# Storing the context's two half-precision parts in the first attention and loading them in the last stage

## What is computed

```python
x = x + jnp.tanh(g_xattn[0]) * _L0_xattn_ref(_layernorm(x, axis=-1), ctx_4096, L0_xattn_Wq, L0_xattn_Wk, L0_xattn_Wv, L0_xattn_Wo)
x = x + jnp.tanh(g_ffn[0]) * _L0_ffn_ref(_layernorm(x, axis=-1), L0_ffn_weight_scales, L0_ffn_weight_q)
x = x + jnp.tanh(g_xattn[1]) * _L1_xattn_ref(_layernorm(x, axis=-1), ctx_4096, L1_xattn_Wq, L1_xattn_bq, L1_xattn_Wk, L1_xattn_bk)
x = x + jnp.tanh(g_ffn[1]) * _L1_ffn_ref(_layernorm(x, axis=-1), L1_ffn_W, L1_ffn_b, L1_ffn_A, L1_ffn_B, L1_ffn_gate_w, L1_ffn_gate_b)
```

## Time and profile before

| | us |
|---|---|
| median of 3 runs (lowest, highest) | 2219.08 (2218.75, 2219.87) |
| the profiled execution | 2214.46 |
| its span, first to last instruction | 2212.6 |
| TensorE busy in the span | 2039.8 (92%) |
| VectorE, ScalarE, GpSimd busy | 1093.4, 774.5, 705.7 |
| `ctx_raw` loads | 32 of 1500.0 KB |
| HBM read, written | 170.49 MB, 51.65 MB |

### The profile page before, as it was taken

The page is one execution under the profiler, slowest core; times in us unless marked ns, Lnnn a source line. Parts: engine busy times, 40 slices in busy tenths (PEclk is TensorE's granted clock), DMA queues, the critical chain, the costliest instruction groups (busy, mean ns, idle before and its releaser), DMA issues. The chain is left out here.

```text
span 2212.6 us, 33544 instructions
## 1 busy us (share of the span) xinstructions
PE 2039.8 (92%) x11792; PEld 1189.2 (54%) x11792; DVE 1093.4 (49%) x2004; ACT 774.5 (35%) x1552; POOL 705.7 (32%) x708
## 2 busy tenths in 40 slices
PE   7989999997999999999999959999999847999998
PEld 3456666654555556555555524444444425665665
DVE  4544444454455555545555633344344427566554
ACT  3422222221455555555555621111111124334431
POOL 0000000011455556555556520000000035665752
PEclk9999999999999999999999979999999969999999
DMA  5423333334124222242222352232232165565561
GB/s 170 143 85 92 88 88 90 87 96 103 35 71 102 63 59 62 62 103 65 62 62 67 97 157 62 61 86 71 57 85 72 64 180 175 184 205 187 172 215 52
DMA packets 331369, 223.21 MB, mean 101 GB/s; under 512 B 295152, under 2 KB 301040, under 8 KB 327072
## 3 DMA queue, kind: packets, MB, share of 16 engines
q1 hardware_dynamic: 244224, 195.36, 31.0%
q10 hardware_dynamic: 87072, 26.89, 5.1%
HBM read 170.49 MB, written 51.65 MB: 100 GB/s over the span
## 5 line engine op out<-in xcount | busy, mean ns | idle before, releaser
L816 POOL TENSOR_TENSOR b_probT<-b_exp,b_probT 128x448 f16<-128x448 f32 (+2 forms) x256 | 265.4, 1040 | 308.8 <-ACT b_probT L879 308.8
L404 POOL TENSOR_TENSOR cT<-ctx_raw,cT 128x375 f16<-128x375 f32 x256 | 220.2, 881 | 135.4 <-ACT cT L399 135.4
L634 PE MATMUL a_pr<-proj_q_p,a_yT 128*128 128x384 f16 x1344 | 228.5, 329 | 2.5 <-DVE a_yT L554 2.5
L946 DVE TENSOR_REDUCE b_nmax<-b_mx_ps 112x2 f16<-112x974 f32 x128 | 149.6, 1168 | 123.9 <-PE b_mx_ps L1027 123.9
L1015 PE MATMUL b_kv_ps<-wkv_p,cT 128*128 128x384 f16 (+1 forms) x1152 | 210.8, 325 | 0.0
L1011 PE MATMUL b_kv_ps<-cT,wkv_p 128*128 128x375 f16 x1152 | 199.6, 324 | 9.0 <-PEq L412 9.0
L1052 PE MATMUL b_s_ps<-b_qT,b_kT 96*128 96x448 f16 (+5 forms) x768 | 188.9, 353 | 2.2 <-DMA b_qT<-b_nrow 2.2
L1067 PE MATMUL b_o_ps<-b_probT,b_v 128*128 128x448 f16 (+5 forms) x768 | 187.3, 351 | 3.1 <-POOL b_probT L816 3.1
L877 ACT ACTIVATE b_exp<-b_s_ps 128x448 f32<-128x448 f32 (+2 forms) x256 | 138.1, 540 | 143.6 <-PE b_s_ps L1052 137.5
L634 PEld LDWEIGHTS a_pr<-proj_q_p,a_yT 128*128 128x128 f16 x1344 | 130.3, 99 | 87.1 <-issue 5.9
L1702 PE MATMUL d_f_ps<-d_w_p,d_y3T 128*112 128x512 f16 x768 | 175.8, 383 | 0.0
(11 more groups left out here) (191 smaller groups left out, 2977.6 us busy)
## 6 DMA issues: line engine op xcount, KB each, us to landing
ctx_raw<-in_ctx_t SPq DMA_DIRECT2D x32, 1500.0 KB, 7.8
d_cn_raw<-in_ctx_nat SPq DMA_DIRECT2D x32, 512.0 KB
qk_scratch<-a_heads ACTq DMA_DIRECT2D x28, 480.0 KB, 6.5
b_qT<-qk_scratch SPq DMA_DIRECT2D x32, 336.0 KB, 4.1
o_scratch<-b_o SPq DMA_DIRECT2D x128, 84.0 KB, 1.9
c_oT<-o_scratch SPq DMA_DIRECT2D x28, 384.0 KB, 5.0
d_cn_raw<-in_ctx_nat SPq DMA_DIRECT2D x16, 476.0 KB
x_scratch<-c_x SPq DMA_DIRECT2D x14, 512.5 KB, 4.6
```

The costliest lines, as they stand in the source:

```text
L404: pool.tensor_tensor(cT[:, p, 1, k, 0:S], ctx_raw[:, k, :], cT[:, p, 0, k, 0:S], ALU.subtract).then_inc(split_lo, 1)
L634: last = mm(pr[:, c % 3, 0:KW], yT[:, p, a, k, :], weight(b, k, c), start=(n == 0 and k == 0), stop=(n == 2 and k == KD - 1))
L816: pool.tensor_tensor(pT[0:m, c, 1, :], ex[0:m, i % 2, :], pT[0:m, c, 0, :], ALU.subtract).then_inc(p_lo, 1)
L946: dve.tensor_reduce(nmax[:, 2 * t:2 * t + 2], mx_ps[0:Q, :, 0:SA], AX.X, ALU.max, negate=True).then_inc(topped, 1)
```

## The change

A scratch array `ct_s` of the shape (batch, partition, part, chunk, 375) in fp16 is added. In stage b, SyncE begins each slot with `store_parts`: once batch b is split it writes both parts of its `cT` buffer to `ct_s` (1.5 MB). ScalarE and GpSimd wait for that store before they write the split of batch b+2 into the same buffer. In stages c and d nothing of the context is split for `cT`: `load_parts` reads the two fp16 parts of a batch from `ct_s` straight into `cT`, for batches 0 and 1 at the head of stage c, and for batch s+1 in slot s of stage d, behind a wait for the scores of batch s-1, which read that buffer last. TensorE waits for that load (`ct_loaded`) where it waited for `split_lo`.

```diff
@@ stage b @@
+                    def load_parts(sp, p, b):
+                        sp.dma_start(cT[:, p, :, :, 0:S].rearrange("p l k s -> p (l k) s"),
+                                     ct_s[bass.ds(b, 1), :, :, :, :].rearrange("b p l k s -> p (b l k) s")).then_inc(ct_loaded[p], 16)
...
+                        def store_parts(j, p, b):
+                            sp.wait_ge(split_lo, KD * (b + 1))
+                            sp.dma_start(ct_s[bass.ds(b, 1), :, :, :, :].rearrange("b p l k s -> p (b l k) s"),
+                                         cT[:, p, :, :, 0:S].rearrange("p l k s -> p (l k) s")).then_inc(ct_stored[p], 16)
                         def slot(j, p, b):
+                            store_parts(j, p, b)
                             load_row(p, b, 1)
...
                             if k == 0:
                                 wait(pool, kv_done, 6 * (b - 1))
+                                pool.wait_ge(ct_stored[p], 16 * (j + 1))
...
@@ stage c @@
                     load(0, 1, 1)
+                    for b in range(2):
+                        load_parts(sp, b, b)
...
-                        if isinstance(s, int) and s == SLOTS - 2:
-                            load_raw(sp, B, 0)
...
-                        if isinstance(s, int) and s == SLOTS - 2:
-                            for k in range(KD):
-                                split_low(pool, 0, B, k)
...
@@ stage d @@
-                load_raw(sp, B + 1, 1)
...
-                            load_raw(sp, s + 1 + B, s + 1)
+                            sp.wait_ge(scored, s)
+                            load_parts(sp, 1 - p, s + 1)
                             load_rows(1 - p, s + 1)
...
-                    if inside(s + 1, B):
-                        for k in range(KD):
-                            split_low(pool, 1 - p, s + 1 + B, k)
...
-                    if inside(s + 1, B):
-                        wait(act, scored, s)
-                        for k in range(KD):
-                            split_high(act, 1 - p, s + 1 + B, k)
...
-                        pe.wait_ge(split_lo, KD * (s + 1 + B))
+                        pe.wait_ge(ct_loaded[p], 16 * (j + 1))
```

More of the change, by code:

```diff
@@ L114, in build @@
     x2_s = nc.dram_tensor("x2_scratch", [R, D + 4], F32).ap()
+    ct_s = nc.dram_tensor("ct_scratch", [B, P, 2, KD, S], F16).ap()
     w4_s = nc.dram_tensor("w4_scratch", [P, KD * D], BF16).ap()
@@ L384, in build @@
                     raw_loaded = nc.alloc_semaphore(name="b_raw_loaded")
+                    ct_stored = [nc.alloc_semaphore(name=f"b_ct_stored{i}") for i in range(2)]
+                    ct_loaded = [nc.alloc_semaphore(name=f"d_ct_loaded{i}") for i in range(2)]
                     split_hi, split_lo = nc.alloc_semaphore(name="b_split_hi"), nc.alloc_semaphore(name="b_split_lo")
@@ L802, in _, with split_piece @@
                             sp.wait_ge(o_stored[i], 32 * B * KV // 2)
+                            sp.wait_ge(ct_stored[i], 16 * B // 2)
                     @block.gpsimd
                     def _(pool):
-                        def split_piece(p, b, k):
+                        def split_piece(j, p, b, k):
                             if k == 0:
                                 wait(pool, kv_done, 6 * (b - 1))
+                                pool.wait_ge(ct_stored[p], 16 * (j + 1))
                             split_low(pool, p, b, k)
@@ L837, in slot @@
                                 if SPLIT_AT <= i < SPLIT_AT + KD and inside(b + 2, B):
-                                    split_piece(p, b + 2, i - SPLIT_AT)
+                                    split_piece(j, p, b + 2, i - SPLIT_AT)
                         run_slots(pool, slot, B)
@@ L844, in _, with split_piece @@
                     def _(act):
-                        def split_piece(p, b, k):
+                        def split_piece(j, p, b, k):
                             if k == 0:
                                 wait(act, kv_done, 6 * (b - 1))
+                                act.wait_ge(ct_stored[p], 16 * (j + 1))
                             split_high(act, p, b, k)
@@ L1227, in slot @@
                             act.activation(y2T[:, 0, :], tr32, ACT.Copy).then_inc(y2T_hi, 1)
-                        if isinstance(s, int) and s == SLOTS - 2:
-                            for k in range(KD):
-                                split_high(act, 0, B, k)
                     run_slots(act, slot, SLOTS, 4)
```

## The result

The changed kernel takes 2229.52 us (median of 5 runs, 2227.41 to 2232.87) against 2219.08 us (5 runs, 2217.76 to 2223.2): ratio 1.0045, 95% interval 1.003 to 1.006. Timed again beside 27 runs of the kernel before it gave 1.0033, 1.0019 to 1.0046. So it is slower by 7 to 10 us, above the range of the prediction (2211.5 to 2225.0), and its sign is wrong. The profiled execution shown here is 15.5 us longer than the one of before (2229.97 to 2214.46); its span is 2228.2.

A forecast was written before the change was run, and what follows sets the result against it. TensorE was taken to bound the kernel: busy through stage b, held by its own gaps in d. Terms -1.7 - 1.0 + 0.1 = -2.6 us took the median 2219.08 to 2216.5 us, with a range of 2211.5 to 2225.

The forecast's parts named there:

- (1): Stages c and d: removing sixteen second splits, beside TensorE's work, is worth 0 in c and in steady slots of d.
- (2): Stage d, slot 9: TensorE's wait for `d_y` goes, as the root is done earlier; worth 1.7 us.
- (3): Stage d, slot 2: the collision stays, but root, subtractions and `d_y` come sooner; worth 1.0 us.
- (5): Stage d: loading `cT` in 750-byte runs takes 4.4 us, 0.8 more (ends 0 and 2.7); costs 0.1 us in slot 3.
- (6): Stage b: each slot's store takes 4.4 to 6.2 us, within 7.1 us of cover before ScalarE reads `ctx_raw`; worth 0.
- slow-store rival: Stage b: a store over 7.1 us loses the excess in each of 14 slots, up to 2259 us; chance 0.05.
- (4): Start of stage d: 1.5 MB less to load while the DMA engines are crowded; worth 0.
- (7): Stage c: two loads of parts, 12.8 us, ahead of tile 2's load fit into 37 us; worth 0.

The follow-up runs named there:

- e1: The kernel before with only the store of the parts added in all 16 slots of stage b; 14.4 us slower than the kernel before, ratio 1.007.
- e4: The changed kernel with the second half of the row of maxima loaded ahead of the parts' store in each slot of stage b; 2236.35 us, ratio 1.0087.

## Why the prediction was wrong

**(1) The removed splits, worth 0 in c and in steady slots: right.** Stage c is 394.0 us in all traces, and the slots of d are 23.17 us apart as before.

**(2) and (3), the waits for `d_y`: right for slot 2, in part chance for slot 9.** Stage d gave 3.5 us for 2.7. In slot 2 of the changed kernel the collision stays, as said, and is met earlier; in slot 9 it is gone, since the root is done at once and the natural context comes later. VectorE, ScalarE, GpSimd and TensorE there, to be compared with the earlier trace rows:

```profile
1876.76 6.70 DVE L104 TENSOR_SCALAR d_y<-d_x,d_norm_mean_var,d_norm_rstd 112x1024 f32<-112x1024 f32 x1 [0.74 <-POOL d_norm_rstd L99]
...
1883.51 0.98 PE L1736 MATMUL d_tr<-ident,d_y 112*128 112x112 f32 x8 [0.74 <-DVE d_y L104]
...
2039.55 0.55 POOL L99 TENSOR_TENSOR d_norm_rstd<-d_norm_var_eps,neg_half 112x1 f32<-112x1 f32 x1 [9.61 <-DVE d_norm_var_eps L94]
...
2040.21 0.81 DVE L104 TENSOR_SCALAR d_y<-d_x,d_norm_mean_var,d_norm_rstd 112x1024 f32<-112x1024 f32 x1 [0.74 <-POOL d_norm_rstd L99]
...
2042.51 2.95 ACT L1516 ACTIVATE d_cn<-d_cn_raw 128x1024 f16<-128x1024 f32 x3 [9.10 <-DMA d_cn_raw<-in_ctx_nat]
...
2047.03 0.92 ACT L1530 ACTIVATE d_y3T<-d_tr 128x896 f16<-128x896 f32 x1 [1.57 <-PE d_tr L1736]
```

Slot 2 gave 0.97 us (1.0 in the sum), slot 9 gave 1.9 (1.7). The rest came in small steps, 0.3 of it in the slot behind slot 9. But the wait in slot 9 is missing in e1 too, where nothing in d was changed. So its 1.9 us are not always there to be gained; slot 2's are, as all three traces with splits in d have that wait at 1.71.

**(5) The load in d: right in its effect, wrong in its size.** Issue to landing is 8.6 us in the steady slots (`ctx_raw`: 8.2), not 4.4. I had taken the rate of a transfer for its time to landing, though the profile of before had that time for its neighbour. The growth of 0.4 us is inside the ends that were given (0 and 2.7). ScalarE's margin ahead of `d_y3T` is 1.57 us in this slot, against the 3.17 in the earlier trace rows, and the slots did not grow, as the forecast had it.

**(6) The store in b: the step that failed, twice.** First its price: "At 248 GB/s it takes 6.2 us, by the same line as above 4.4". It took 12.7, so 121 GB/s, half of the 240 of the slower end used for the line. I had drawn a line by run length through rows that could not show what sets the price, the starting address: the 256-byte stores start on multiples of 256 by the shape of their array, and the row at 240 GB/s was of loads; the loads of the parts turned out not to care. The rule that I did cite, of boundaries at 256 bytes (the Trainium skill, DMA: Bandwidth & Descriptors, How a descriptor splits into AXI transactions), gave an estimate of 17% and was weighed for the load alone. For the store it is not the rule seen here, since starts at multiples of 64 (7.5 us) are as fast as at multiples of 768 (7.4 us).

Second its place. The cover was worked out for "all 14 slots with a load", and the other two slots were taken at 0 without being worked out. The slots that have no context load are 14 and 15, and these hold the whole loss: one has ScalarE's own loads, waited for in order in the middle of its exponentials, and the other has short steps. Step (6) listed what stands behind the store in SyncE's queue, but the DMA engines are shared with ScalarE's queue, and the trace of before had ScalarE waiting 0.6 to 2.1 us for six of those seven loads already, which is no cover at all. The 14 slots, where the slow-store rival had placed 43 us, lost nothing: past the 7.1 us of cover comes another 3.05 us for which ScalarE may wait (e4).

That rival named the cause and got 0.05. From its threshold of 7.1 us the loss would have been 5.6 us in each of 14 slots, 78 us; it came to 12 us in two. Neither its price nor its place held.

**(4) and (7): right.** The start of d moved by 0.4 us, and c is as long as before.

**Stages and medians.** The stages give +8.2 us against the two traces of before, and the medians 10.4 and 6.7. Over all twelve comparisons the medians lie above the stages' sum by 1 to 5 us in ten. Why is open: the start column is left out of the sums and scatters by more, one trace holds one draw of slot 9's wait and of the stretches at half clock, and no run here separates these.

## What to carry to other kernels

Before a tensor is written to scratch, look at the addresses at which its runs start: the change from a pitch of 750 bytes to 768 is one number, and it took the store from 12.7 to 7.4 us. When a transfer is added to every slot of a loop, go to the slots that differ, the last ones above all, and ask there which loads of other queues it meets and which engine waits for them in order. A wait that is seen on a helper engine is not yet a loss; how much more it bears is its own number, and a variant that goes over it, as e4 does, gives it slot by slot.

## What the runs showed of the hardware

- A store from on-chip to device memory of 1.5 MB in runs of 750 bytes takes 12.7 us to landing when they start at multiples of 750, 11.7 at multiples of 752 (16), 10.4 at 800 (32), 7.5 at 832 (64), 7.4 at 768 (256), and 5.4 as runs of 12,032 bytes. All in the same slots of the same kernel, with the row, queries, keys and the next context behind it. Why 64 is the grain, no run here shows.
- The load of the same bytes is indifferent to it: 8.6 to 9.1 us by the median of all 16 loads, whatever the pitch or the run.
- While the slow store is in flight the DMA share is not lower than in the fast one (1.13 against 1.06) but the bytes are (181 against 294 GB/s): a full share says nothing on the work done.
- In the slot with a hole of 5.2 us TensorE was granted 0.50 of its clock for 6.8 us in all, so slot 14 lost more than the hole: 8.4 us. The kernel before had none of this in one trace and 3.4 us of it in the other, behind a wait of 2.12 us that both traces have.
